# A transformer block on one core: the weights prepared in pieces of 1 MB, and the first token tile in the same stage

## The chip, the cores and the metric

The kernel runs on one core of a Trainium2 chip. The core has five engines that each work through a queue of their own: TensorE (PE, with its weight load PEld), VectorE (DVE), ScalarE (ACT), GpSimd (POOL) and SyncE (SP), which here issues the DMAs. Engines wait for each other by semaphores. The metric is the device time of one execution in microseconds (us), the median of three runs.

## What is computed

A layer norm of x (8 x 1024 x 512), an attention branch on it with 16 heads, a feed-forward branch with ternary weights, and the sum of x and both:

```python
def ternarize_weights(w):
    gamma = jnp.mean(jnp.abs(w))
    return jnp.sign(jnp.round(w / (gamma + EPS))) * gamma
def bitlinear(x, w):
    xn = layer_norm(x)
    ...
    return jnp.einsum('bsd,od->bso', x_hat, w_hat)
...
xn = _layernorm(x, axis=-1)
x = x + _L0_attn_ref(xn, L0_attn_W_qkv, L0_attn_W_o) + _L0_ffn_ref(xn, L0_ffn_w_fc, L0_ffn_w_proj)
```

W_qkv is 1536 x 512 (3 MB), W_o 512 x 512 (1 MB), w_fc 2048 x 512 and w_proj 512 x 2048 (4 MB each), all float32. A ternary weight is 1 above a threshold (gamma + EPS)/2, -1 below its negative, and 0 between, so a matrix can be made ternary only when the mean of its absolute values is known.

## The kernel before

The program is three stages, one after the other, each a block that all engines enter and leave together (a barrier stands between two blocks): `weight_stage`, `token_stage`, `attention_output_stage`.

`weight_stage` (lines 84 to 270) prepares four matrices. SP loads each with one DMA, in the order W_qkv, w_fc, w_proj, W_o (lines 121 to 124). W_qkv: DVE takes the largest absolute value of each partition (line 159), POOL that over the partitions (`partition_all_reduce`, line 147), DVE makes a scale of it (lines 163, 164). PE transposes 128 x 128 blocks, four to a unit of 512 columns in PSUM (line 221), ACT writes the unit as float16 into `wh` (line 255), DVE the rest into `wl` (`low_parts`, line 175). There are 12 units and four PSUM buffers. For the ternary matrices DVE sums the absolute values of w_fc (line 182) and ACT those of w_proj (line 259); POOL adds the partitions; DVE makes the thresholds (lines 185 to 187) and then two passes over the whole matrix, one that compares with the lower threshold (line 190) and one that compares with the upper and subtracts the first result (line 191). Then PE transposes the result, 64 blocks to a matrix (line 228), and ACT copies the 16 units of each to `t1T` and `t2T` (lines 263, 266). W_o is treated as W_qkv was (lines 202 to 210, 242, 270), and at the end PE sums `t2T` over its rows into `colsum` with 16 matmuls against ones (line 247), which DVE copies out (line 212).

`token_stage` (from line 274) works through 16 tiles of 512 tokens. Ahead of its loop it prepares the first tile by itself: SP loads it (line 347), DVE makes its statistics (`stats`, lines 419 to 424), POOL turns them into factors in nine short steps (`norm`, lines 384 to 392), DVE normalises the rows into `x2` (`normed`, line 432), PE transposes them (line 606), ACT writes the high part `xh` (`high`, line 535) and DVE the low part `xl` (`low`, line 448). The second and later tiles are prepared inside the loop's body for the tile before. The body begins on PE with the products of `t1T` and the tile (line 640), then those for q, k and v (line 616), the products of `t2T` (line 652), and so on. `attention_output_stage` follows, with its own buffers.

The order on every engine is the order in which its function is written. What stands in one of these queues waits for all that stands ahead of it.

## Time and profile before

| | us |
|---|---|
| median of 3 runs | 3440.56 |
| lowest, highest | 3439.92, 3441.74 |
| the profiled execution's own time | 3441.16 |
| its span in the profile | 3439.4 |
| PE busy in the span | 3313.1 (96%) |
| DVE, ACT, POOL busy | 2424.7, 1989.6, 1966.8 |
| last instruction of the weight stage (DVE) begins | 78.81 |
| first matmul of the first tile's body (PE) begins | 101.16 |

The profile counts time from the span's start. "Busy" is the time in which an engine works on at least one instruction. A row of a timeline begins with the start and the duration, and ends with the idle time of that engine before it and what ended it. The granted clock of PE is given as a share of 2.4 GHz: 1.00 is 2.4 GHz, 0.50 is 1.2 GHz.

### The profile page before, as it was taken

The page shows a single profiled execution, that of the slowest core. Times are in us where ns is not written, and L with a number is a line of the kernel's source. Part 1 is how long each engine was busy: PE and PEld are TensorE (multiplying, and loading weights), DVE is VectorE, ACT ScalarE, POOL GpSimd, SP SyncE. Part 2 cuts the span into 40 slices and gives each one's busy share as a digit, 9 for nine tenths or more (in the row PEclk, how much of TensorE's full clock was granted, in tenths as well). Part 3 has the DMA queues.
Part 4 walks back from the last instruction along what each step waited for, and adds up shares of the span by engine and source line. Part 5 has one row for each costly group of instructions (what it writes and reads, how often), then busy time and mean ns, then how long its engine had stood idle before and what let it go on. Part 6 is the DMA issues. An engine that isn't in the chain of part 4 may idle for free.

```text
span 3439.4 us, 47929 instructions
## 1 busy us (share of the span) xinstructions
PE 3313.1 (96%) x17648; PEld 1371.8 (40%) x17648; DVE 2424.7 (70%) x3450; ACT 1989.6 (58%) x2949; POOL 1966.8 (57%) x690
## 2 busy tenths in 40 slices
PE   3899999999999999989999999999999999999788
PEld 2444444444444444442333333333333333333233
DVE  6676666666666666668787777877877878776144
ACT  3444444444444444433787777877877878778411
POOL 0322232323232323223999999999999999999600
PEclk8899999999999999996999999999999999999999
DMA  4122222222222222224333333332333333331277
GB/s 169 71 71 94 84 87 78 89 89 89 78 82 94 85 82 78 86 71 84 71 72 79 76 74 71 78 77 67 83 72 67 85 70 67 85 73 42 92 261 255
DMA packets 375958, 307.64 MB, mean 89 GB/s; under 512 B 300672, under 2 KB 317056, under 8 KB 365440
## 3 DMA queue, kind: packets, MB, share of 16 engines
q1 hardware_dynamic: 375744, 304.69, 31.9%
q8 instruction: 146, 2.39, 0.3%
q14 instruction: 68, 0.56, 0.1%
HBM read 96.99 MB, written 139.46 MB: 69 GB/s over the span
## 4 chain that ended last, share of the span: by engine, by line
PE 46%; DMA 3%; DVE 2%; issue 1%; POOL 1%; ACT 1%; SPq 0%; POOLq 0%; ACTq 0%; DVEq 0%
PE es_for_maxima_and_scores L1058 14%; PE outputs L1049 14%; PE es_for_maxima_and_scores L1037 13%; PE misc L1082 5%; DMA k_stackT<-attention_scratch 2%; DMA out<-q_stackT 2%; DVE half_maxima L973 1%; POOL probs_sum L894 1%; PE es_for_maxima_and_scores L1115 1%; DVE q_stackT L1009 0%; ACT k_stackT L932 0%; ACT probs L926 0%; DVE q_stackT L1015 0%; DMA q_stackT<-stack_scratch 0%; PE misc L1066 0%
## 5 line engine op out<-in xcount | busy, mean ns | idle before, releaser
L973 DVE TENSOR_REDUCE half_maxima<-es_for_maxima_and_scores 128x1 f32<-128x512 f32 x2048 | 1275.6, 682 | 324.4 <-PE es_for_maxima_and_scores L1058 324.3
L926 ACT ACTIVATE probs<-es_for_maxima_and_scores,scalars 128x512 f32<-128x512 f32 x2048 | 1253.6, 692 | 379.7 <-PE es_for_maxima_and_scores L1037 377.2
L894 POOL TENSOR_TENSOR probs_sum<-probs_sum,probs 128x2048 f32<-128x2048 f32 x256 | 1164.0, 4547 | 27.8
L1058 PE MATMUL es_for_maxima_and_scores<-k_stackT,q_stackT 96*128 96x512 f16 x2048 | 800.4, 392 | 12.1 <-DMA q_stackT<-stack_scratch 11.1
L1037 PE MATMUL es_for_maxima_and_scores<-q_stackT,k_stackT 98*128 98x512 f16 x2048 | 778.2, 383 | 5.9 <-ACT probs L926 4.5
L1049 PE MATMUL outputs<-probs,v_rows 128*32 128x512 f32 x4096 | 541.1, 600 | 3.1 <-ACT probs L926 0.8
L402 POOL TENSOR_TENSOR gelu_sum<-gelu_sum,gelu_out 128x1024 f32<-128x1024 f32 x96 | 254.8, 2654 | 451.5 <-ACT gelu_out L577 451.5
L1058 PEld LDWEIGHTS es_for_maxima_and_scores<-k_stackT,q_stackT 96*128 96x128 f16 x2048 | 199.7, 98 | 603.9 <-DVE half_maxima L973 447.4
L640 PE MATMUL psA<-x_hi,ternary_fcT 128*128 128x512 f16 x1024 | 389.9, 381 | 1.4 <-DVE x_lo L448 1.4
L640 PE MATMUL psA<-x_lo,ternary_fcT 128*128 128x512 f16 x1024 | 389.8, 381 | 0.0
L652 PE MATMUL psC<-ternary_projT,h_lo 128*128 128x512 f16 x1024 | 388.0, 379 | 0.0
L652 PE MATMUL psC<-ternary_projT,h_hi 128*128 128x512 f16 x1024 | 388.0, 379 | 0.0
L894 POOL TENSOR_TENSOR probs_sum<-probs 128x2048 f32<-128x2048 f32 x64 | 291.2, 4550 | 154.5 <-ACT probs L926 154.5
L1037 PEld LDWEIGHTS es_for_maxima_and_scores<-q_stackT,k_stackT 98*128 98x128 f16 x2048 | 294.8, 145 | 211.9 <-ACT probs L926 31.6
L577 ACT ACTIVATE gelu_out<-psA,scalars 128x1024 f32<-128x1024 f32 x128 | 142.7, 1115 | 347.9 <-PE psA L640 347.9
L402 POOL TENSOR_TENSOR gelu_sum<-gelu_out 128x1024 f32<-128x1024 f32 x16 | 41.0, 2564 | 489.5 <-ACT gelu_out L577 489.5
L471 DVE TENSOR_SCALAR h_hi<-gelu_out,scalars 128x1024 f16<-128x1024 f32 x128 | 186.5, 1457 | 161.0 <-ACT gelu_out L577 157.3
L616 PE MATMUL psB<-wqkvT_hi,x_hi 128*128 128x512 f16 x768 | 291.1, 379 | 0.0
L616 PE MATMUL psB<-wqkvT_lo,x_hi 128*128 128x512 f16 x768 | 291.1, 379 | 0.0
L616 PE MATMUL psB<-wqkvT_hi,x_lo 128*128 128x512 f16 x768 | 291.1, 379 | 0.0
L557 ACT ACTIVATE hi_hi_lo_hi_rows<-psB,qkv_scale 128x1024 f16<-128x1024 f32 x192 | 214.0, 1115 | 127.2 <-PE psB L616 127.2
L535 ACT CAST x_hi<-psB 128x512 f16<-128x512 f32 x64 | 34.5, 588 | 335.6 <-PE psB L606 335.6
(126 smaller groups left out, 3175.8 us busy)
## 6 DMA issues: line engine op xcount, KB each, us to landing
stack_scratch<-hi_hi_lo_hi_rows SPq DMA_DIRECT2D x32, 1536.0 KB, 5.1
stack_scratch<-hi_hi_lo_hi_rows SPq DMA_DIRECT2D x32, 576.0 KB, 6.0
v_scratch<-v_rows_out SPq DMA_DIRECT2D x32, 576.0 KB, 6.9
x_rows<-in_L_attn_x SPq DMA_DIRECT2D x16, 1024.0 KB, 4.8
x_plus_ffn_scratch<-x_rows SPq DMA_DIRECT2D x16, 1024.0 KB, 3.9
v_rows<-v_scratch SPq DMA_DIRECT2D x32, 512.0 KB, 4.0
inverse_denominators<-denominators_scratch SPq DMA_DIRECT2D x256, 64.0 KB, 2.0
attention_scratch<-out_normed SPq DMA_DIRECT2D x64, 256.0 KB, 2.1
```

The costliest lines, as they stand in the source:

```text
L402: nc.gpsimd.tensor_tensor(gacc[:], g[:, 0, :] if j == 1 else gacc[:], g[:, j % 4, :], ALU.add).then_inc(g_added, 1)
L471: nc.vector.tensor_scalar(hh[:, pair, :], gj, S["inv1"], None, ALU.mult).then_inc(hh_ready, 1)
L557: nc.scalar.activation(stack[:, i % 2, heads, 0:2, :], rows.unsqueeze(2).to_broadcast([P, BANK // DH, 2, DH]), ACT.Copy, scale=rc[:, s, i: ...
L616: last = nc.tensor.matmul(psB[:, u % 2, :], xx[:, s, c, i * P:(i + 1) * P], keep[ww][:, c, cols], start=(k == 0), stop=(k == len(terms) - 1))
L640: last = nc.tensor.matmul(psA[:, 2 * (j % 2) + b, :], w, xx[:, s, c, :], start=(c == 0 and k == 0), stop=(c == CD - 1 and k == 1))
L652: last = nc.tensor.matmul(psC[:, i % 2, :], h[:, f, i * P:(i + 1) * P], keep["t2T"][:, f, :], start=(f == 0 and k == 0), stop=(f == CF - 1 ...
L894: nc.gpsimd.tensor_tensor(acc[:, hf], pr[:, 0] if j == 1 else acc[:, hf], pr[:, j], ALU.add).then_inc(added, 1)
L926: nc.scalar.activation(pr[:, w % 8, h, :], psS[:, bank(g, HG * w + h), :], ACT.Exp, scale=keep["scal"]["escale"]).then_inc(exp_done, 1)
L973: nc.vector.tensor_reduce(mx[:, slot(n, 2), h, t, kh:kh + 1], psX[:, bank(n, r), :], axis=AX.X, op=ALU.max).then_inc(max_done, 1)
L1037: nc.tensor.matmul(psS[:, bank(g, HG * w + h), :], kT[0:AUG, slot(g, 4), h, i:L:KT_N], qT[0:AUG, slot(g, 4), h, hf * BANK:(hf + 1) * BANK] ...
L1049: last = nc.tensor.matmul(psO[32 * h:32 * h + 32, :], v[:, slot(g, 2), h, i, :], pr[:, w % 8, h, :], start=(i == 0), stop=(i == KT_N - 1))
L1058: nc.tensor.matmul(psX[:, bank(n, r), :], qT[0:STACK, slot(n, 4), h, t * P:(t + 1) * P], kT[0:STACK, slot(n, 4), h, kh * BANK:(kh + 1) * B ...
```

## The change

**Loads.** W_qkv and w_fc come in pieces of 1 MB, each with a semaphore of its own; the first tile of x is loaded between them into `xs`, which with `xh`, `xl`, `bn`, `mv`, `sm`, `rc` and their semaphores now lives in `keep` through both stages. W_o and w_proj (four pieces) are issued only when PE has transposed all of W_qkv, because W_o and the normalised tile `x2` take the place of W_qkv's rows.

**W_qkv.** The largest absolute value is taken piece by piece; the units run in the order of the pieces.

**The first tile.** Its statistics stand on DVE after six of the twelve low parts, its factors on POOL after the first reduction over partitions, its transposes on PE behind the W_qkv units, its high part on ACT and its low part on DVE between pieces of w_fc. The same code is taken out of `token_stage`.

**Sums.** ACT sums the absolute values of both matrices, in eight pieces; DVE adds four partial sums of each.

**Ternary weights.** DVE no longer subtracts. Two comparisons of a piece give two float16 indicators: `above` (a buffer of its own, used for both matrices) and `below` (written over the float32 piece that it is made of, 4 x 512 with gaps). PE makes the transposed difference in PSUM: for each block a matmul of `above` with the identity and one of `below` with the negative identity, accumulated. PSUM for it is float32.

**Column sums.** They are interleaved with w_proj's units, two behind.

```diff
+            for k in range(THIRDS):
+                sp.dma_start(wqkv[:, piece(k)], rows[:, piece(k)]).then_inc(ld_qkv[k], 16)
+            sp.dma_start(xs[:, 0], x_v[0]).then_inc(x_loaded[0], 16)
...
+            sp.wait_ge(full32, N32)
+            sp.dma_start(wo, W_o.rearrange("(j p) d -> p j d", p=P)).then_inc(ld_o, 16)
...
-                link(nc.vector.tensor_scalar(tern_rows, flat, thr[:, thr0 + 1:thr0 + 2], None, ALU.is_lt))
-                nc.vector.scalar_tensor_tensor(tern_rows, flat, thr[:, thr0:thr0 + 1], tern_rows,
-                                               ALU.is_gt, ALU.subtract).then_inc(tern, 1)
...
+            def fc_piece(k):
+                nc.vector.tensor_scalar(above[:, piece(k), :], wfc[:, piece(k), :], thr[:, 1:2], None, ALU.is_gt)
+                nc.vector.tensor_scalar(fc_below[:, piece(k), :], wfc[:, piece(k), :], thr[:, 0:1], None,
+                                        ALU.is_lt).then_inc(tern, 1)
...
+                for r in range(4):
+                    nc.tensor.matmul(pst[:, u % 3, r * P:(r + 1) * P], plus[r], id16[:], start=True, stop=False)
+                    last = nc.tensor.matmul(pst[:, u % 3, r * P:(r + 1) * P], minus[r], nid16[:], start=False, stop=True)
                 last.then_inc(full16, 1)
...
+            for f in range(CF):
+                k, q = divmod(f, 4)
+                if q == 0:
+                    pe.wait_ge(tern, 4 + k + 1)
...
+                difference(CF + f, [above[:, 4 * k + r, cols] for r in range(4)], [proj_below[:, r, k, cols] for r in range(4)])
+                if f >= 2:
+                    column_sum(f - 2)
+            column_sum(CF - 2)
+            column_sum(CF - 1)
```

In `token_stage` the first tile's load, `norm(0, 0)`, `stats(0, 0)`, `normed(0, 0)`, `low`, `high` and `transposes` ahead of the loop go.

What stands on DVE from the low parts of W_qkv to the second matrix, before:

```order
L175 SCALAR_TENSOR_TENSOR wqkvT_lo<-weight_psum,scalars,wqkvT_hi 128x512 [waits hi_out] x11
L182 TENSOR_REDUCE per_partition<-wfc_rows 128x1 [waits loaded_fc]
L185 TENSOR_SCALAR scalars<-over_partitions 128x1 [waits reduced]
L186 TENSOR_SCALAR thresholds<-scalars 128x1 [waits vector_step]
L187 TENSOR_SCALAR thresholds<-thresholds 128x1 [waits vector_step]
L190 TENSOR_SCALAR ternary_fc_rows<-wfc_rows,thresholds 128x8192 [waits vector_step]
L191 SCALAR_TENSOR_TENSOR ternary_fc_rows<-wfc_rows,thresholds,ternary_fc_rows 128x8192 [waits vector_step]
```

The same place now; `wqkv_rows` in row L256 is `x2`, and `wfc_rows` as an output is `below`:

```order
L203 SCALAR_TENSOR_TENSOR wqkvT_lo<-weight_psum,scalars,wqkvT_hi 128x512 [waits hi_out] x6
L256 TENSOR_SCALAR wqkv_rows<-tile_xs,tile_mv,tile_sm 128x512 [waits mv_ready,pool_step]
L256 TENSOR_SCALAR wqkv_rows<-tile_xs,tile_mv,tile_sm 128x512 x3
L208 TENSOR_REDUCE per_partition_sums<-per_partition 128x1 [waits parts]
L211 TENSOR_SCALAR scalars<-over_partitions 128x1 [waits reduced]
L212 TENSOR_SCALAR thresholds<-scalars 128x1 [waits vector_step]
L213 TENSOR_SCALAR thresholds<-thresholds 128x1 [waits vector_step]
L216 TENSOR_SCALAR above_threshold<-wfc_rows,thresholds 128x2048 [waits vector_step]
L217 TENSOR_SCALAR wfc_rows<-wfc_rows,thresholds 128x4x512
L216 TENSOR_SCALAR above_threshold<-wfc_rows,thresholds 128x2048
L217 TENSOR_SCALAR wfc_rows<-wfc_rows,thresholds 128x4x512
L265 TENSOR_TENSOR tile_xl<-weight_psum,tile_xh 128x512 [waits xh_ready] x4
```

The sum of absolute values has left DVE, the tile's normalising stands ahead of the thresholds, and its low part between the second and the third piece.

ACT in the whole weight stage, before:

```order
L255 ACTIVATE wqkvT_hi<-weight_psum,scalars 128x512 [waits full32] x11
L259 ACTIVATE ternary_proj_rows,per_partition<-wproj_rows 128x8192 [waits loaded_proj]
L263 COPY ternary_fcT<-weight_psum 128x512 [waits full16] x16
L266 COPY ternary_projT<-weight_psum 128x512 [waits full16] x16
L270 ACTIVATE woT_hi<-weight_psum,wo_scale 128x512 [waits wo_full,wo_scaled]
L270 ACTIVATE woT_hi<-weight_psum,wo_scale 128x512 [waits wo_full] x3
```

And now, from the last units of W_qkv on:

```order
L352 ACTIVATE wqkvT_hi<-weight_psum,scalars 128x512 [waits full32] x4
L356 ACTIVATE above_threshold,per_partition<-wfc_rows 128x2048 [waits loaded_fc1]
L356 ACTIVATE above_threshold,per_partition<-wfc_rows 128x2048 [waits loaded_fc2]
L356 ACTIVATE above_threshold,per_partition<-wfc_rows 128x2048 [waits loaded_fc3]
L380 CAST tile_xh<-weight_psum 128x512 [waits t_full] x4
L368 CAST ternary_fcT<-ternary_psum 128x512 [waits full16] x8
L363 ACTIVATE wqkv_rows,per_partition<-wproj_rows 128x2048 [waits loaded_proj0]
L363 ACTIVATE wqkv_rows,per_partition<-wproj_rows 128x2048 [waits parts,loaded_proj1]
L368 CAST ternary_fcT<-ternary_psum 128x512 [waits full16] x8
L363 ACTIVATE wqkv_rows,per_partition<-wproj_rows 128x2048 [waits parts,loaded_proj2]
L363 ACTIVATE wqkv_rows,per_partition<-wproj_rows 128x2048 [waits parts,loaded_proj3]
L392 ACTIVATE woT_hi<-weight_psum,wo_scale 128x512 [waits wo_full,wo_scaled]
```

The sums over w_proj, which stood ahead of all the copies of `t1T`, now stand between and behind them, and W_o's high part ahead of the copies of `t2T`.

## Rows read from the trace of the kernel before

**Rows 1.** Page: busy time, share of the span, instructions of each engine.

```profile
PE 3313.1 (96%) x17648; PEld 1371.8 (40%) x17648; DVE 2424.7 (70%) x3450; ACT 1989.6 (58%) x2949; POOL 1966.8 (57%) x690
```

**Rows 2.** Stretches: length, busy PE, PEld, DVE, ACT, POOL; PE clock, DMA share, GB/s.

```profile
0.00:79.50 79.50, 28.38 (x208) 21.16 (x208) 58.11 (x41) 34.06 (x51) 5.88 (x18) 0.81 0.42 158
295.00:502.00 207.00, 207.00 (x993) 97.89 (x992) 143.11 (x156) 94.63 (x107) 66.01 (x40) 1.00 0.27 90
```

**Rows 3.** Timeline from W_qkv's landing to the first sum; start, duration, engine, line.

```profile
12.21 6.55 DVE L159 TENSOR_REDUCE per_partition<-wqkv_rows 128x1 f32<-128x6144 f32 x1 [12.21 <-DMA wqkv_rows<-in_L_attn_W_qkv]
...
18.90 0.38 POOL L147 PARTITION_ALL_REDUCE over_partitions<-per_partition  x1 [16.43 <-DVE per_partition L159]
...
20.50 8.62 DVE L175 SCALAR_TENSOR_TENSOR wqkvT_lo<-weight_psum,scalars,wqkvT_hi 128x512 f16<-128x512 f32 x12 [0.27 <-ACT wqkvT_hi L255]
...
25.02 3.00 ACT L255 ACTIVATE wqkvT_hi<-weight_psum,scalars 128x512 f16<-128x512 f32 x5 [0.17 <-PE weight_psum L221]
...
29.04 8.68 DVE L182 TENSOR_REDUCE per_partition<-wfc_rows 128x1 f32<-128x8192 f32 x1
```

**Rows 4.** Timeline, the sum on ACT and the passes over both matrices on DVE.

```profile
32.98 7.03 ACT L259 ACTIVATE ternary_proj_rows<-wproj_rows 128x8192 f16<-128x8192 f32 x1 [4.96 <-DMA wproj_rows<-in_L_ffn_w_proj]
...
38.81 4.49 DVE L190 TENSOR_SCALAR ternary_fc_rows<-wfc_rows,thresholds 128x8192 f16<-128x8192 f32 x1
...
43.33 8.75 DVE L191 SCALAR_TENSOR_TENSOR ternary_fc_rows<-wfc_rows,thresholds,ternary_fc_rows 128x8192 f16<-128x8192 f32 x1
...
57.20 8.75 DVE L191 SCALAR_TENSOR_TENSOR ternary_proj_rows<-wproj_rows,thresholds,ternary_proj_rows 128x8192 f16<-128x8192 f32 x1
```

**Rows 5.** Timeline, the second matrix's transposes, copies and column sums.

```profile
66.00 3.53 PEld L228 LDWEIGHTS weight_psum<-id,ternary_proj_rows 128*128 128x128 f16 x32 [6.48 <-DVE ternary_proj_rows L191]
...
66.65 7.93 ACT L266 COPY ternary_projT<-weight_psum 128x512 f16<-128x512 f16 x16 [5.93 <-PE weight_psum L228]
...
75.15 3.62 PE L247 MATMUL colsum_psum<-ternary_projT,ones 128*128 128x512 f16 x16
75.20 2.73 DVE L209 SCALAR_TENSOR_TENSOR woT_lo<-weight_psum,wo_scale,woT_hi 128x512 f16<-128x512 f32 x4 [5.59 <-ACT woT_hi L270]
78.81 0.69 DVE L212 COPY ternary_proj_sums<-colsum_psum 128x512 f32<-128x512 f32 x1 [0.88 <-PE colsum_psum L247]
```

**Rows 6.** Timeline, the first token tile's preparation and the body's start.

```profile
79.78 0.34 SPq L347 DMA_DIRECT2D x_rows<-in_L_attn_x  x1
...
85.08 2.47 DVE L419 BATCH_NORM_STATS2 bn<-x_rows 128x6 f32<-128x512 f32 x4 [5.58 <-DMA x_rows<-in_L_attn_x]
...
89.17 0.19 POOL L384 TENSOR_TENSOR norm_small<-mean_var,powers_and_epsilons 128x4 f32<-128x4 f32 x1 [20.00 <-issue]
...
93.30 1.91 DVE L432 TENSOR_SCALAR x_normed<-x_rows,mean_var,norm_small 128x512 f32<-128x512 f32 x4 [5.34 <-POOL qkv_scale L392]
...
101.16 0.61 PE L640 MATMUL psA<-x_hi,ternary_fcT 128*128 128x512 f16 x1 [1.40 <-DVE x_lo L448]
...
107.48 0.38 PE L616 MATMUL psB<-wqkvT_hi,x_hi 128*128 128x512 f16 x1
108.83 0.75 DVE L471 TENSOR_SCALAR h_hi<-gelu_out,scalars 128x1024 f16<-128x1024 f32 x1 [7.73 <-ACT gelu_out L577]
```

**Rows 7.** Stretches of 2 or 3 us, columns as in rows 2.

```profile
66.00:68.00 2.00, 1.99 (x19) 1.77 (x20) 1.93 (x4) 1.35 (x3) 0.00 (x0) 0.50 0.00 0
...
70.00:72.00 2.00, 1.63 (x19) 0.90 (x16) 0.00 (x0) 2.00 (x6) 0.00 (x0) 1.00 0.00 0
...
101.00:104.00 3.00, 2.84 (x7) 1.04 (x8) 0.10 (x1) 0.68 (x1) 0.00 (x0) 0.50 0.00 0
```

**Rows 8.** Line 353, loads of tiles 2 to 16: issue (ns, first and last start), landing.

```profile
L353 SPq DMA_DIRECT2D x_rows<-in_L_attn_x x15: 340/372/425, 80.2 to 1366.7; - x15
...
DMA to landing us min/median/max: 4.7/4.8/7.3
```

**Rows 9.** Line 147: the changes of POOL's configuration ahead of the all-reduces.

```profile
L147 POOLq MODIFY_POOL_CONFIG  x2: 11/11/11, 2.4 to 2.4; - x2
```

More of the change, by code:

```diff
@@ L80, in wait, with weight_stage @@
         eng.wait_ge(sem, value)
-def weight_stage(nc, W_qkv, W_o, w_fc, w_proj, keep):
+def weight_stage(nc, x_v, W_qkv, W_o, w_fc, w_proj, keep):
     n_w = F * D
@@ new lines, in _ @@
+            last.then_inc(mv_ready, 1)
+            for u in range(6, N32):
+                low_part(u)
+            dve.wait_ge(pool_step, 9)
+            dve.wait_ge(mv_ready, 1)
+            for i in range(4):
+                last = nc.vector.tensor_scalar(x2[:, i, :], xs[:, 0, i, :], mv[:, i, 0:1], sm[:, 6, i:i + 1],
+                                               ALU.subtract, ALU.mult)
+            last.then_inc(x2_ready, 1)
+            thresholds(FC, 4, S["gamma1"], 2, 4)
+            fc_piece(0)
@@ new lines, in _ @@
+            fc_piece(1)
+            for c in range(CD):
+                dve.wait_ge(xh_ready, c + 1)
+                nc.vector.tensor_tensor(xl[:, 0, c, :], ps[:, c, :], xh[:, 0, c, :], ALU.subtract).then_inc(xl_ready, 1)
+            fc_piece(2)
+            fc_piece(3)
+            dve.wait_ge(ld_o, 16)
+            nc.vector.tensor_reduce(sums[:, 2:3], wo, axis=AX.XY, op=ALU.max, apply_absolute_value=True).then_inc(summed, 1)
+            thresholds(PROJ, 12, S["gamma2"], 4, 8)
+            proj_piece(0)
@@ L267, in _ @@
+            for u in range(8):
+                fc_out(u)
+            proj_sum(0)
+            proj_sum(1)
+            for u in range(8, CF):
+                fc_out(u)
+            proj_sum(2)
+            proj_sum(3)
             act.wait_ge(wo_scaled, 1)
@@ L588, in body @@
                     high(shift(t, 1), 1 - s, range(CD))
-            high(0, 0, range(CD))
             steps(act, body)
@@ L659, in body @@
                         transposes(shift(t, 1), 1 - s, (2 * i - 2, 2 * i - 1))
-            transposes(0, 0, range(CD), first=True)
             steps(pe, body)
```

281 lines of the change are left out of this document (171 added, 110 removed).

## The prediction, made before the changed kernel had run

> **What bounds the kernel now.** I read the page first: PE is busy 96% of the span [rows 1], so DVE's 70% tells little. The stretches say where some of the missing 4% is: in a stretch of over two token tiles PE is busy 207.0 of 207.0 us at full clock, in the first 79.5 us only 28.4 [rows 2]. The change touches nothing but the time before the first tile's body, which begins at 101.16. Behind that PE does not stop in the token stage, so an earlier start passes on to the end one for one. The timeline gives the chain that sets the 101 us. W_qkv lands at 12.2; DVE reduces it for 6.55 us, then works without a real pause to 66: low parts 8.62, sum of w_fc 8.68 [rows 3], then 4.49 + 8.75 us for each ternary matrix [rows 4]. After 66 come PE's transposes with ACT's copies, W_o, the column sums to 78.77, DVE's last copy to 79.50 [rows 5]. Then the first tile starts from nothing: load 5.3, statistics, 5.34 us of waiting for POOL, normalising, transposes: 21.7 us in which nothing else runs [rows 6].
>
> **The change part by part** (times are those of the profiled execution, from its start).
>
> Head. The large loads land at a pace. W_qkv ends a wait at 12.2, w_proj one at 33.0, with 8 MB between them: 2.6 us for each 1 MB. Counted from 12.2 the pieces of W_qkv land near 7.0, 9.6, 12.2, then x at 14.8 and w_fc at 17.4, 20.0, 22.6, 25.2 [rows 3, 4]. DVE needs 6.55/3 = 2.2 us for a piece and ends at 14.4 instead of 18.76. From that end to the first low part it was 1.74 us; with one more small sum of 0.15 the low parts begin at 16.3, 4.2 earlier.
>
> Low parts and the tile. Six low parts (8.62/12 = 0.72 each) to 20.7, statistics 2.5 plus some 0.6 for the aggregates to 23.9, six more to 28.3. POOL's factors take 5.3 us from the statistics [rows 6], to 29.2, under the low parts; normalising 1.9, to 31.1. ACT has the high parts (0.60 each, five in 3.00 [rows 3]) and the sum over w_fc's first piece; it is free near 27. A sum over 8192 columns was 7.03 us [rows 4]; over 2048 that is 1.76 and a fixed part, 2.0. Three more: 33.0. So DVE waits 2 us for ACT, and normalising is free. The tile's transposes on PE (from 31.1) and its four high parts on ACT (behind the sums, to about 36) end before the first piece of w_fc is ready, and cost nothing.
>
> First thresholds. From the end of DVE's sum (37.72) to the first pass (38.81) lay 1.09 us [rows 3, 4]; with the small sum the first comparison begins at 34.3.
>
> Comparisons. 8192 columns took 4.49, 1024 took 0.75 [rows 4, 6], so 2048 take 0.75 + 1024 x 0.00052 = 1.28 us, 1.23 back to back: 2.45 a piece, 19.6 for eight. Before, the two passes of both matrices were 26.5 and DVE's sum 8.7. That is the size of the idea: 15.6 us less on DVE, against 64 + 64 more small matmuls on PE. w_fc's pieces are ready at 36.8 and 39.2, then the tile's low parts (4 x 0.7, hidden, as will be seen), 44.5 and 46.9; W_o's maximum to 49.2.
>
> ACT becomes the bound. Its queue now is: 8 copies of `t1T`, two sums over w_proj, 8 copies, two sums. The eighth copy needs piece 2 (39.2) and PE. A weight load of 128 columns comes each 3.53/32 = 0.11 us at 1.2 GHz [rows 5, 7]; a unit of 8 matmuls is 0.88 us there and half of that, 0.44, at 2.4 GHz. The eighth copy ends at 41.7 (fast) to 44.5 (slow); I take 43.0. Then 4.0 (two sums), 4.8 (8 x 0.60; before, from float16 PSUM, 7.93/16 = 0.50 [rows 5], but the float32 row is the nearer one), 4.0: 55.8. w_proj's pieces are issued when PE has finished W_qkv, about 26.2; 5.3 us for W_o [rows 6] and 2.6 for each piece give 42.0 for the last, so their late issue is hidden by 10 us.
>
> Second thresholds at 55.8 + 0.2 + 1.1 = 57.1. DVE: four pieces 9.8, W_o's scale 0.5, W_o's low parts 2.7 [rows 5]: last piece at 70.1. ACT copies `t2T` from 62.6 on (W_o's high parts are ahead of it), 16 x 0.60 = 9.6, to 72.2 at the earliest. PE does a unit and a column sum in 0.44 + 0.22 = 0.66, so behind the last piece 4 x 0.66 = 2.6, a copy 0.67, two column sums 0.6, DVE's copy 0.73 [rows 5]: stage end 74.7; I take 75.0 instead of 79.5. Only 4.5 us: the 15.6 saved on DVE come back as ACT's sums and a longer chain of copies.
>
> Passage to the token stage. DVE's end to SP's first DMA was 0.28 us, the shortest it can be [rows 5, 6]; POOL's first step there began 1.2 us after the statistics that it waited for (89.17 against 93.30 - 5.34 = 87.96) [rows 6]. I take 0.9 of 0.3 to 1.5. PE begins the body at 75.9 instead of 101.16: 25.3.
>
> Clock. The 16 matmuls from 101.16 to 107.48 took 6.3 us, at 1.2 GHz [rows 6, 7]; at 2.4 GHz 16 x 0.216 = 3.5 (the column sums: 15 in 3.62 - 0.38 [rows 5]). PE will have worked almost without a gap from 63 to 74, and in the like place before it had reached 1.00 four us after it began and kept it [rows 7]. That gives 2.8 more, and would not if it fell. The Trainium skill (TensorE: Matmul & The Clock Gate, HAM clock gate) says that the low clock is the default state and that activity releases it. By that page the added matmuls help, and the row agrees (0.50 in 66 to 68, 1.00 in 70 to 72).
>
> **Sum:** 25.3 + 2.8 = 28.1 us off 3441.16, which is 3413.1 by the profiled execution; the median stands 0.6 below that one, 3412.5. I round to 3413.
>
> Against the pieces speaks the Trainium skill (DMA: Bandwidth & Descriptors, Anatomy of one DMA), which puts a fixed cost of about 2 us on each DMA; there are 9 more in this stage, x's among them. The trace shows two DMAs of 1 MB issued 0.4 us apart that landed 5.3 and 7.3 us after issue [rows 6, 8], 2.4 us apart, no more than the pace of the large ones. Paid one behind another it would be 4 us on W_qkv's last piece, and the sum would be 24 instead of 28; by the row it is nothing.
>
> **Rivals.**
> 1. PE's clock stays low where the kernel now leans on it. PE idles between w_fc's last unit (about 52) and w_proj's first (60). Then the eighth copy is 1.5 later, units with their column sum take 1.3 instead of 0.66 from 63 on (13 of them, 17 us, stage end 7.5 later), and the first tile's 2.8 are not won: 28.1 - 1.5 - 7.5 - 2.8 = 16.3, 3424. Against: before, 3.5 us of dense transposes were enough [rows 5, 7]. Chance 0.12.
> 2. The second comparison, written with gaps over its own input, runs at the pace of the two-input pass, 8.75/8192 [rows 4], 2.3 instead of 1.2 us. Two of w_fc's and four of w_proj's lie on the chain: 6.6 later, 3419. No row has such an output. Chance 0.10.
> 3. POOL now changes its configuration three times around the tile's factors. The change before the first all-reduce is issued at 2.4 and the all-reduce runs at 18.90, when its data are there [rows 3, 9], so it may cost anything up to 16.4 us. In the new order it has 4 us between the factors (29.2) and the sum over w_fc (33.2): 0 to 12 later, up to 3425. Chance 0.08.
> 4. The change doesn't shorten the stage: ACT's and PE's hand-overs eat the 4.5 us and it ends at 79.5; the tile alone gives 20.8 + 2.8 = 23.6, 3417. Chance 0.05.
> 5. Slower than before: the tile's buffers lie elsewhere in memory for all 16 tiles. If PE's reads or the writers of `xh`, `xl` became slower by more than 28.1/16 = 1.8 us a tile, the kernel would lose. A tile takes (1366.7 - 80.2)/14 = 92 us [rows 8]: 2% is the point of no gain, 3% would be 3413 + 44 = 3457. Against: the body's code is the same and PE has no idle time in it [rows 2]. Chance 0.03.
>
> **How the numbers follow.** The forecast has 0.62. Its own unknowns: passage 0.3 to 1.5, eighth copy 41.7 to 44.5, clock behind the last piece (4 x 1.3 instead of 4 x 0.66, 2.6 us more): 3409 to 3419. The range 3409 to 3424 takes in rivals 2 and 4, about half of 1 and of 3, and leaves out 5. A measurement of this kernel can tell 0.2%, 7 us. All cases but the fifth are at least 15 us faster: faster 0.96, within 0.2% 0.01, slower 0.03.
>
> **What would show it.** First low part at 16.3; first comparison at 34.3, behind ACT's sum of piece 3; a comparison 1.2 to 1.3 us in both forms; DVE idle from about 49 to 57, ended by ACT's last sum; last comparison at 70; DVE's copy of the column sums ending at 75; body at 76 with matmuls 0.216 apart from the start; the rest shifted as a whole. I am wrong if DVE's second wait is ended by POOL or a DMA, if a comparison lasts over 2 us, or if a token tile's length changes.

## The result, and the profile after

| | before | after |
|---|---|---|
| median of 4 runs each, us | 3440.24 | 3419.32 |
| lowest, highest | 3436.09, 3441.74 | 3417.53, 3421.41 |
| the profiled execution, its span | 3441.16, 3439.4 | 3417.53, 3415.7 |
| ratio of times | | 0.9941 [0.9928, 0.9954] |
| body of the first tile begins on PE | 101.16 | 79.37 |

The kernel is 20.9 us faster, and the interval leaves out no change. The time lies inside the range; it is 6.3 us above the forecast of 3413.0. (The four runs of before are the three of the beginning and one beside the changed kernel.)

The page of after: PE is still what bounds the span; it gained 5 us of busy time by the added matmuls, and DVE lost 17 [rows 1].

```profile
PE 3318.2 (97%) x17776; PEld 1381.0 (40%) x17776; DVE 2407.6 (70%) x3466; ACT 1997.6 (58%) x2963; POOL 1963.7 (57%) x692
```

DVE in the weight stage, after (columns as in [rows 3]). L216 and L222 are the comparisons that give `above`, L217 and L223 those that give `below`, L208 the small sum, L211 the first step of the thresholds, L256 the tile's normalising, L287 the last copy. Comparisons of the later pieces are left out.

```profile
9.18 2.29 DVE L228 TENSOR_REDUCE per_partition<-wqkv_rows 128x1 f32<-128x2048 f32 x1 [0.38 <-DMA wqkv_rows<-in_L_attn_W_qkv]
...
16.17 4.35 DVE L203 SCALAR_TENSOR_TENSOR wqkvT_lo<-weight_psum,scalars,wqkvT_hi 128x512 f16<-128x512 f32 x6 [0.27 <-ACT wqkvT_hi L352]
...
29.09 1.91 DVE L256 TENSOR_SCALAR wqkv_rows<-tile_xs,tile_mv,tile_sm 128x512 f32<-128x512 f32 x4 [1.85 <-POOL tile_rc L185]
31.75 0.16 DVE L208 TENSOR_REDUCE per_partition_sums<-per_partition 128x1 f32<-128x4 f32 x1 [0.75 <-ACT above_threshold L356]
39.10 0.15 DVE L211 TENSOR_SCALAR scalars<-over_partitions 128x1 f32<-128x1 f32 x1 [7.20 <-POOL over_partitions L163]
...
39.66 1.29 DVE L216 TENSOR_SCALAR above_threshold<-wfc_rows,thresholds 128x2048 f16<-128x2048 f32 x1
40.87 1.28 DVE L217 TENSOR_SCALAR wfc_rows<-wfc_rows,thresholds 128x2048 f16<-128x2048 f32 x1
...
60.33 0.16 DVE L208 TENSOR_REDUCE per_partition_sums<-per_partition 128x1 f32<-128x4 f32 x1 [6.42 <-ACT wqkv_rows L363]
...
61.56 1.29 DVE L222 TENSOR_SCALAR above_threshold<-wproj_rows,thresholds 128x2048 f16<-128x2048 f32 x1
...
78.36 0.69 DVE L287 COPY ternary_proj_sums<-colsum_psum 128x512 f32<-128x512 f32 x1 [3.74 <-PE colsum_psum L318]
```

POOL in the same stretch: its first and last step for the tile's factors, and the all-reduce for w_fc.

```profile
24.96 0.19 POOL L177 TENSOR_TENSOR tile_sm<-tile_mv,powers_and_epsilons 128x4 f32<-128x4 f32 x1 [10.02 <-issue]
...
28.85 0.20 POOL L185 TENSOR_TENSOR tile_rc<-tile_sm,powers_and_epsilons 128x4 f32<-128x4 f32 x1
38.67 0.40 POOL L163 PARTITION_ALL_REDUCE over_partitions<-per_partition_sums  x1 [9.61 <-issue]
```

The changes of POOL's configuration ahead of the all-reduces (L163) and of the factors (L177), as their issue is recorded:

```profile
L163 POOLq MODIFY_POOL_CONFIG  x4: 10/10/11, 2.8 to 29.3; - x4
```

```profile
L177 POOLq MODIFY_POOL_CONFIG  x2: 82/82/83, 14.9 to 14.9; - x2
```

What is to be seen: DVE has the sum over w_fc at 31.9, three thresholds' steps from its comparisons, and waits 7.20 us for POOL. POOL does nothing in that time: its all-reduce is released by "issue", not by DVE. Its last factor ends at 29.05, the change is issued at 29.3, and the all-reduce runs 9.4 us after that. The change takes 10 ns in its own row; its cost stands in the next row's idle time. The other change, issued at 14.9 ahead of the factors, cost 10.02 us. Normalising waits for it only from 27.2 to 29.1, but it isn't wholly hidden: the statistics were there at 23.3 and the factors began at 24.96. So the change back was issued some 1.6 us later than it could have been, and these are part of the 7.20.

ACT after that wait, and PE at the start of the first tile's body:

```profile
45.84 2.60 ACT L368 CAST ternary_fcT<-ternary_psum 128x512 f16<-128x512 f32 x5 [0.27 <-PE ternary_psum L313]
48.29 1.95 ACT L363 ACTIVATE wqkv_rows<-wproj_rows 128x2048 f16<-128x2048 f32 x1
...
52.33 3.97 ACT L368 CAST ternary_fcT<-ternary_psum 128x512 f16<-128x512 f32 x8
...
70.00 7.87 ACT L395 CAST ternary_projT<-ternary_psum 128x512 f16<-128x512 f32 x12 [0.63 <-PE ternary_psum L313]
```

```profile
79.37 0.38 PE L750 MATMUL psA<-tile_xh,ternary_fcT 128*128 128x512 f16 x1 [1.05 <-PEq L86]
79.59 0.38 PE L750 MATMUL psA<-tile_xl,ternary_fcT 128*128 128x512 f16 x1
```

ACT copies `t1T` (L368), sums over w_proj (L363), copies again, sums again; DVE's second wait of 6.42 us is for that. Then W_o (L392) and `t2T` (L395). DVE's last copy ends at 79.05 and PE begins the body at 79.37, with matmuls 0.22 apart at once [rows 6: 6.3 us for sixteen; here 3.45].

PE's clock in four stretches (columns as in [rows 2]):

```profile
36.00:41.00 5.00, 0.00 (x0) 0.00 (x0) 1.80 (x5) 0.00 (x0) 0.40 (x1) 0.50 0.77 326
40.00:46.00 6.00, 3.79 (x37) 3.80 (x38) 6.00 (x7) 1.92 (x4) 0.00 (x0) 0.51 0.01 4
66.00:68.00 2.00, 1.55 (x12) 1.01 (x11) 2.00 (x4) 2.00 (x5) 0.00 (x0) 0.50 0.00 0
70.00:72.00 2.00, 2.00 (x28) 1.67 (x27) 2.00 (x3) 1.77 (x4) 0.00 (x0) 1.00 0.00 0
```

PE had nothing to do from 36 to 41 and began w_fc's transposes at 0.51 of full clock, and w_proj's, from 64.1 on, at 0.50.

### The profile page after: what moved, and what is told of

It is laid out like the page before. It is cut to its first block, busy times and chain, and to the rows that moved or that the text cites. A ratio compares the mean times of both kernels' runs of the same rounds, so it can differ in the third digit from the quotient of the medians.

```text
span 3415.7 us, 48244 instructions
## 1 busy us (share of the span) xinstructions
PE 3318.2 (97%) x17776; PEld 1381.0 (40%) x17776; DVE 2407.6 (70%) x3466; ACT 1997.6 (58%) x2963; POOL 1963.7 (57%) x692
## 3 DMA queue, kind: packets, MB, share of 16 engines
q1 hardware_dynamic: 375872, 304.69, 31.9%
## 4 chain that ended last, share of the span: by engine, by line
PE 47%; DMA 3%; DVE 2%; issue 1%; POOL 1%; ACT 1%; SPq 0%; POOLq 0%; ACTq 0%; DVEq 0%
PE es_for_maxima_and_scores L1167 14%; PE outputs L1158 14%; PE es_for_maxima_and_scores L1146 13%; PE misc L1191 5%; DMA k_stackT<-attention_scratch 1%; DMA out<-q_stackT 1%; DVE half_maxima L1082 1%; POOL probs_sum L1003 1%; PE es_for_maxima_and_scores L1224 1%; DVE q_stackT L1118 0%; ACT k_stackT L1041 0%; ACT probs L1035 0%; DVE q_stackT L1124 0%; DMA q_stackT<-stack_scratch 0%; PE misc L1175 0%
## 5 line engine op out<-in xcount | busy, mean ns | idle before, releaser
L1167 PE MATMUL es_for_maxima_and_scores<-k_stackT,q_stackT 96*128 96x512 f16 x2048 | 800.3, 391 | 12.2 <-DMA q_stackT<-stack_scratch 11.2
L750 PE MATMUL psA<-tile_xh,ternary_fcT 128*128 128x512 f16 x1024 | 388.2, 379 | 1.3 <-PEq L86 1.1
L750 PE MATMUL psA<-tile_xl,ternary_fcT 128*128 128x512 f16 x1024 | 388.1, 379 | 0.0
L726 PE MATMUL psB<-wqkvT_lo,tile_xh 128*128 128x512 f16 x768 | 291.1, 379 | 0.0
L726 PE MATMUL psB<-wqkvT_hi,tile_xl 128*128 128x512 f16 x768 | 291.1, 379 | 0.0
L726 PE MATMUL psB<-wqkvT_hi,tile_xh 128*128 128x512 f16 x768 | 291.1, 379 | 0.0
L668 ACT ACTIVATE hi_hi_lo_hi_rows<-psB,tile_rc 128x1024 f16<-128x1024 f32 x192 | 213.8, 1113 | 127.4 <-PE psB L726 127.4
L646 ACT CAST tile_xh<-psB 128x512 f16<-128x512 f32 x60 | 32.2, 588 | 314.5 <-PE psB L716 314.5
```

Of the source, the lines that this page charges most:

```text
L668: nc.scalar.activation(stack[:, i % 2, heads, 0:2, :], rows.unsqueeze(2).to_broadcast([P, BANK // DH, 2, DH]), ACT.Copy, scale=rc[:, s, i: ...
L726: last = nc.tensor.matmul(psB[:, u % 2, :], xx[:, s, c, i * P:(i + 1) * P], keep[ww][:, c, cols], start=(k == 0), stop=(k == len(terms) - 1))
L750: last = nc.tensor.matmul(psA[:, 2 * (j % 2) + b, :], w, xx[:, s, c, :], start=(c == 0 and k == 0), stop=(c == CD - 1 and k == 1))
L1167: nc.tensor.matmul(psX[:, bank(n, r), :], qT[0:STACK, slot(n, 4), h, t * P:(t + 1) * P], kT[0:STACK, slot(n, 4), h, kh * BANK:(kh + 1) * B ...
```

## The experiments

The question was what the missing 3.5 us of the body's start are: the forecast was 75.9. The comparison that opens the chain is 5.4 us late, and a change of POOL's configuration stands in front of it. The runs take that change apart (1 to 3), then the other parts of the change (4 to 6), and then use what was found (7, 8). Runs 1, 2, 3 and 5 were made together with the kernel before at 3439.39 (one run), the others with it at 3438.79 (nine runs). A time without an interval is that of one run, and is read together with its trace.

### 1. w_proj's loads behind the all-reduce

```diff
+            sp.wait_ge(reduced, 2)
             rows = w_proj.rearrange("(j p) f -> p j f", p=P)
             for k in range(4):
```

> w_proj's four loads wait until POOL has added w_fc's sums over the partitions, so no DMA traffic runs between W_o's landing (about 31) and that all-reduce. In the changed kernel POOL's configuration change is issued at 29.3 and the all-reduce runs at 38.67, while its data are there at 31.9 and the DMA queue is full until 39. Theory A (a configuration change takes a fixed 9 to 10 us): the all-reduce runs at 38 to 39 again. Theory B (its code waits behind w_proj's packets in the DMA queues): the all-reduce runs at 31.9 to 33. Under either the body begins later than 79.4, since w_proj lands late: under A w_proj's last piece at about 38.7 + 13 = 52, which ACT's last sum (58.3) still hides, so the body at 79 to 81; under B at about 74.

Measured: 3414.48 us, the body at 79.20. (The time is 3.1 us below the profiled execution of the changed kernel, with a body that begins only 0.2 earlier; the rest lies in the attention stage and the projection, whose code is the same. One run doesn't show that the edit did it.) The queues of DMA, first in the changed kernel from 29.3 to 38.8, then here from 30 to 37 (a digit is the busy share of the 16 DMA engines in a fortieth of the window):

```profile
DMA  9999989998899999988999999979999899979999
```

```profile
DMA  1000000000000000000000000000000000000000
```

And POOL's last factor and its all-reduce here:

```profile
30.17 0.20 POOL L186 TENSOR_TENSOR tile_rc<-tile_sm,powers_and_epsilons 128x4 f32<-128x4 f32 x1
36.31 0.40 POOL L164 PARTITION_ALL_REDUCE over_partitions<-per_partition_sums  x1 [5.94 <-issue]
```

With the DMA engines idle the all-reduce comes 5.94 us after the last factor instead of 9.61. So neither pure case holds: 5.9 us belong to the change of configuration itself, and 3.7 go with the traffic beside it, w_proj's four pieces. The first comparison is at 37.32, only 2.3 us earlier than after, because the change ahead of the factors took 11.32 us here instead of 10.02. And the body begins only 0.2 earlier. The gain is lost behind the comparison:

```profile
43.49 0.59 ACT L369 CAST ternary_fcT<-ternary_psum 128x512 f16<-128x512 f32 x1 [0.27 <-PE ternary_psum L314]
44.34 0.59 ACT L369 CAST ternary_fcT<-ternary_psum 128x512 f16<-128x512 f32 x1 [0.27 <-PE ternary_psum L314]
```

ACT's copies of `t1T` stand 0.85 us apart, each waiting for PE at half clock, up to the seventh (in the changed kernel up to the fourth), and three more do so in the second half. ACT's last sum ends at 60.0 against 60.3. PE's pause ahead of these copies was shorter than in the changed kernel (4.0 us instead of 7.5), and the half clock behind it lasted longer; the traces don't say why.

### 2. The totals of both ternary matrices on PE

```diff
-            reduce(FC, bass.bass_isa.ReduceOp.add)
             reduce(2, bass.bass_isa.ReduceOp.max)
-            reduce(PROJ, bass.bass_isa.ReduceOp.add)
...
-                dve.wait_ge(reduced, summed_to)
+                dve.wait_ge(pe_total, summed_to)
...
+            def add_partitions(k):
+                pe.wait_ge(summed, k + 1)
+                nc.tensor.matmul(psw[:, k:k + 1], ones_sq[:], sums[:, k:k + 1], start=True, stop=True).then_inc(pe_total, 1)
```

`ones_sq` is 128 x 128 ones in float32; the product gives every partition the sum over all. The matmul for w_fc stands behind the first unit of the tile's transposes, that for w_proj ahead of its first unit.

> The sums of both ternary matrices are added over the partitions by one float32 matmul with ones on PE; POOL keeps the two maxima, so its second configuration change has from 29 to 54 to finish. Theory (the all-reduce for w_fc is what was late): first comparison at about 33.0 instead of 39.66, since the sum is ready at 31.91 and matmul, PSUM read and three small steps take about 1.1. The chain behind it on ACT moves up with it, 6 to 6.7 us, so the body begins at 72.7 to 73.4 instead of 79.37. Rival (something else in the chain, such as ACT's sums over w_proj waiting for their DMA, takes over): first comparison at 33 but ACT's sums end less than 3 us earlier than 60.3 and the body begins at 76 or later. w_proj's last piece lands at 39, before ACT would ask for it at about 51, so I expect the first.

Measured: 3408.99 us, the body at 72.21, 7.2 earlier than after. DVE, and the stretch 36 to 41:

```profile
32.93 0.16 DVE L211 TENSOR_SCALAR scalars<-colsum_psum 128x1 f32<-128x1 f32 x1 [0.68 <-PE colsum_psum L304]
...
33.50 1.29 DVE L216 TENSOR_SCALAR above_threshold<-wfc_rows,thresholds 128x2048 f16<-128x2048 f32 x1
...
54.44 1.29 DVE L222 TENSOR_SCALAR above_threshold<-wproj_rows,thresholds 128x2048 f16<-128x2048 f32 x1
```

```profile
36.00:41.00 5.00, 3.92 (x64) 3.58 (x64) 5.00 (x7) 4.06 (x10) 0.00 (x0) 1.00 0.83 347
```

The total is there 0.68 us after the small sum, and the first comparison begins at 33.50, 6.2 us earlier. That is 0.8 before the forecast's 34.3. The other 1.0 us goes with PE: it passes from the tile's transposes to w_fc's with little pause, the clock is 1.00 where it was 0.51, and ACT ends its first eight copies 7.6 us after the first comparison instead of 8.8. The rival, by which ACT's sums would hold the body at 76 or later, is out.

### 3. Six changes of configuration with nothing beside them

```diff
             reduce(PROJ, bass.bass_isa.ReduceOp.add)
+            for n in range(3):
+                nc.gpsimd.tensor_tensor(extra[:, 4 * n:4 * n + 4], keep["powers"][:, 4:8], keep["powers"][:, 4:8], ALU.add)
+                nc.gpsimd.partition_all_reduce(extra[:, 12 + n:13 + n], sums[:, 0:1], P, bass.bass_isa.ReduceOp.max)
```

The results go to a tile that nothing reads.

> Behind POOL's last all-reduce stand three more pairs of an ordinary step on 128x4 and an all-reduce on 128x1, into a scratch tile that nothing reads, in the stretch from 61 on in which no DMA runs. Theory A (each change of configuration takes 9 to 10 us by itself): starts of the six steps lie about 9 to 10 us apart, 55 to 60 us in all, and the token stage begins that much later than the other engines need (body at about 120). Theory B (a change is short unless DMA traffic delays it): the six steps lie under 2 us apart, and the body begins at 79 to 80. A mixed outcome would be one direction short and one long.

Measured: 3441.86 us, the body at 104.40, since the stage can't end before POOL. POOL, the all-reduce for w_fc and then the added chain:

```profile
40.32 0.40 POOL L164 PARTITION_ALL_REDUCE over_partitions<-per_partition_sums  x1 [9.60 <-issue]
...
70.24 0.19 POOL L192 TENSOR_TENSOR extra<-powers_and_epsilons 128x4 f32<-128x4 f32 x1 [7.63 <-issue]
76.22 0.38 POOL L193 PARTITION_ALL_REDUCE extra<-per_partition_sums  x1 [5.78 <-issue]
...
97.21 0.19 POOL L192 TENSOR_TENSOR extra<-powers_and_epsilons 128x4 f32<-128x4 f32 x1 [6.65 <-issue]
103.68 0.38 POOL L193 PARTITION_ALL_REDUCE extra<-per_partition_sums  x1 [6.27 <-issue]
```

Both forms of the expectation were wrong: a change is neither short nor 9 to 10 us. Each is issued 0.4 us after the start of the instruction before it; to an ordinary step it costs 6.7 to 7.6 us of idle time, to an all-reduce 5.8 to 6.3. In the stretch with w_proj's traffic it is 9.60 again, and 11.63 to the tile's factors under w_fc's. The Trainium skill (GPSIMD Engine Reference, Instruction dispatch) says that the first call of a freshly loaded kernel pays a load of code of about 6 us that no row of a profile shows; the all-reduces of this chain agree, with 5.8 to 6.3, and the ordinary steps lie above it, with 6.7 to 7.6. That the time grows under traffic is what runs 1 and 3 show beside it. It would if the code came through the same DMA engines; that it does isn't shown.

PE stood idle for 24 us ahead of this body, and its first matmuls are 0.43 apart. From the body's start to the attention stage it took 1448.3 us, against 1446.6 in the changed kernel: so a start at half clock costs 1.7 us here (2.3 by the kernel before, with 1448.9), where the forecast had 2.8.

### 4. DVE subtracts, in pieces

```diff
-                nc.vector.tensor_scalar(above[:, piece(k), :], wfc[:, piece(k), :], thr[:, 1:2], None, ALU.is_gt)
-                nc.vector.tensor_scalar(fc_below[:, piece(k), :], wfc[:, piece(k), :], thr[:, 0:1], None,
-                                        ALU.is_lt).then_inc(tern, 1)
+                link(nc.vector.tensor_scalar(above[:, piece(k), :], wfc[:, piece(k), :], thr[:, 0:1], None, ALU.is_lt))
+                nc.vector.scalar_tensor_tensor(above[:, piece(k), :], wfc[:, piece(k), :], thr[:, 1:2], above[:, piece(k), :],
+                                               ALU.is_gt, ALU.subtract).then_inc(tern, 1)
```

The same for w_proj; PE then makes one matmul for each block instead of two.

> The changed kernel with the ternary matrices made as before, by two passes of DVE that end in a subtraction, but still piece by piece (a comparison of 1.28 us and a two-input pass of 2048 x 8.75/8192 = 2.2 to 2.3), and one matmul for each block on PE instead of two. Theory (DVE's time for a piece lies on the chain for six of the eight pieces, PE's added matmuls lie beside it): w_fc's pieces end about 3.5 apart instead of 2.4; ACT's last sum over w_proj ends at about 62 instead of 60.3; the four pieces of w_proj add 4 x 1.1; PE's units are shorter, 0.44 with a column sum instead of 0.66, which gives back about 1. The body begins at 83 to 85 instead of 79.37. Rival (what PE pays eats what DVE saves): the body begins at 78.5 to 80.5. POOL's configuration change can move either by up to 2.

Measured: 3424.73 us, the body at 88.42, 9.0 later than after (1.0 of it is a first comparison at 40.67, behind changes of 10.68 and 9.82 us). DVE, and the last stretch of the stage:

```profile
40.67 1.29 DVE L216 TENSOR_SCALAR above_threshold<-wfc_rows,thresholds 128x2048 f16<-128x2048 f32 x1
42.00 2.35 DVE L217 SCALAR_TENSOR_TENSOR above_threshold<-wfc_rows,thresholds,above_threshold 128x2048 f16<-128x2048 f32 x1
...
87.40 0.69 DVE L287 COPY ternary_proj_sums<-colsum_psum 128x512 f32<-128x512 f32 x1 [4.08 <-PE colsum_psum L317]
```

```profile
78.00:87.40 9.40, 7.09 (x42) 3.96 (x42) 5.22 (x7) 4.50 (x8) 0.00 (x0) 0.64 0.00 0
```

A piece takes 3.58 us instead of 2.40, the old pair of passes made 3.3 of it by [rows 4]. That is most of it. From the first comparison of w_fc to ACT's last sum it takes 2.9 us more than in the changed kernel, and from the first comparison of w_proj to the end of DVE's last piece (82.9) 4.8 more, with DVE at work throughout. The stretch that is left, from there to DVE's copy, takes 4.5 us against 4.2. The body is still 3 to 5 us behind what was expected: 1.0 is POOL's, the sums are 1.2 later than was reckoned, and the shorter units of PE, which were to give back 1, gave nothing. Most of ACT's copies of `t2T` from 73.5 on start 0.85 us behind the one before, the last at 86.13; the clock granted from 78 to 87.4 is 0.64, where the changed kernel has 1.00 for its last copies. So the added matmuls, besides sparing DVE a slow pass, came with a higher clock, but little of the 9.0 us is the clock's. Whether the number of matmuls or the shorter pauses went with it isn't separated by this run.

### 5. The first tile prepared in the token stage, as before

```diff
-            sp.dma_start(xs[:, 0], x_v[0]).then_inc(x_loaded[0], 16)
             rows = w_fc.rearrange("(j p) d -> p j d", p=P)
...
-            pool.wait_ge(mv_ready, 1)
-            link(nc.gpsimd.tensor_tensor(v1, var, keep["powers"][:, 4:8], ALU.add))
...
+            norm(0, 0)
             steps(pool, body)
```

Also the tile's steps on DVE, PE and ACT go back; the pieces and the indicators stay.

> The changed kernel with the first tile prepared in the token stage, as in the kernel before; the pieces and the difference on PE stay. Theory A: without the tile's factors there is no configuration change between POOL's all-reduces, so w_fc's all-reduce runs when its data are ready. ACT's sums move up by about 1 us (DVE's statistics no longer between the low parts), so the first comparison at about 32.5; DVE has no low parts of x between pieces. Stage end 79.05 - 7 = 71 to 72. Then the tile costs what it did, 101.16 - 79.50 = 21.7, so the body begins at 92.5 to 94 at the lower clock: 7 to 9 us earlier than before, 13 to 15 later than with the tile inside, that is about 3433. If instead the all-reduce is late again, near 38, Theory A is wrong.

Measured: 3429.80 us, the body at 94.13, 3 us less than was expected. DVE (L190 is the first step of the thresholds, L501 the normalising), and the body:

```profile
32.03 0.15 DVE L190 TENSOR_SCALAR scalars<-over_partitions 128x1 f32<-128x1 f32 x1 [0.53 <-POOL over_partitions L162]
...
71.74 0.69 DVE L248 COPY ternary_proj_sums<-colsum_psum 128x512 f32<-128x512 f32 x1 [3.57 <-PE colsum_psum L273]
77.75 2.47 DVE L488 BATCH_NORM_STATS2 tile_bn<-tile_xs 128x6 f32<-128x512 f32 x4 [5.31 <-DMA tile_xs<-in_L_attn_x]
```

```profile
94.13 0.39 PE L709 MATMUL psA<-tile_xh,ternary_fcT 128*128 128x512 f16 x1 [1.40 <-DVE tile_xl L517]
94.36 0.38 PE L709 MATMUL psA<-tile_xl,ternary_fcT 128*128 128x512 f16 x1
```

The change has two halves of unequal size. The weight stage alone ends at 72.43 instead of 79.50: 7.1 us. The tile inside it brings 94.13 - 79.37 = 14.8. It is less than the 21.7 us that the passage took before [rows 6], because the tile's steps cost the stage 79.05 - 72.43 = 6.6 us there. Without them no ordinary step of POOL stands between the all-reduces, DVE waits 0.53 us for the total instead of 7.20, and the first comparison is at 32.60. The change of configuration is thus a price of moving the tile, and the largest one.

The last two rows show something else. The sixteen matmuls of this body are 0.22 us apart from the second on, at full clock, as in the changed kernel, though the tile is prepared in the token stage as before, PE transposes it from 5.9 us ahead of the body as it did there, with the same pauses of 0.55 us between two halves and 1.40 ahead of the body, and was idle for 16.6 us ahead of all that. In the kernel before the clock stayed at 0.50 until the body had run for nearly 6 us. So the same work of PE ended at either level, and it isn't shown that the full clock at the changed kernel's body, some 2 of its 20.9 us, comes from moving the tile.

### 6. W_qkv and w_fc by one DMA each

```diff
-            for k in range(THIRDS):
-                sp.dma_start(wqkv[:, piece(k)], rows[:, piece(k)]).then_inc(ld_qkv[k], 16)
+            sp.dma_start(wqkv[:], rows).then_inc(ld_qkv[0], 16)
...
-            for k in range(4):
-                sp.dma_start(wfc[:, piece(k)], rows[:, piece(k)]).then_inc(ld_fc[k], 16)
+            sp.dma_start(wfc[:], rows).then_inc(ld_fc[0], 16)
```

> The changed kernel with W_qkv loaded by one DMA of 3 MB and w_fc by one of 4 MB; the reductions stay in three parts, and all else too. Theory: DVE's first reduction begins at 12.2 instead of 6.5, its three parts end at 19.0 instead of 14.15, the first low part begins at 21.0 instead of 16.2. All behind it moves by 4.8: POOL's all-reduce, its change to the ordinary configuration (which takes 7 to 11 us from there and so holds the tile's factors), the factors, the change back. The first comparison at 43.5 to 46 and the body at 83 to 85.5. Rival (the pieces gain nothing because POOL's changes of configuration and ACT's sums set the time later on): the body below 81.

Measured: 3419.55 us, the body at 82.43, 3.1 later. (By the time alone nothing would be seen: it is one run, and lies inside the changed kernel's 3417.53 to 3421.41.) DVE:

```profile
11.99 6.67 DVE L226 TENSOR_REDUCE per_partition<-wqkv_rows 128x1 f32<-128x2048 f32 x3 [11.99 <-DMA wqkv_rows<-in_L_attn_W_qkv]
...
20.68 4.35 DVE L201 SCALAR_TENSOR_TENSOR wqkvT_lo<-weight_psum,scalars,wqkvT_hi 128x512 f16<-128x512 f32 x6 [0.27 <-ACT wqkvT_hi L350]
...
43.23 1.29 DVE L214 TENSOR_SCALAR above_threshold<-wfc_rows,thresholds 128x2048 f16<-128x2048 f32 x1
```

The pieces bring 4.5 us at the first low part (16.17 against 20.68), as the sum had it (4.2). W_qkv's last piece lands at 11.86 in the changed kernel, and the whole matrix at 11.99 here: two more DMAs in front of it cost nothing. Of the 4.5 us the first comparison keeps 3.6 (39.66 against 43.23) and the body 3.1. Both are earlier than was expected (43.5 to 46 and 83 to 85.5): the change ahead of the factors, issued at 19.4, did not hold them. They began at 27.92, released by DVE's statistics after 8.46 us of idle time, so this change took no more than that, though w_fc's load filled the DMA engines until about 24.4.

### 7. One version on top of run 2, and run 2 again

Run 7 is run 2 with w_proj's last piece summed by DVE, which waits at that time, and with W_o's high and low parts moved behind the first eight copies of `t2T`.

```diff
-            thresholds(PROJ, 12, S["gamma2"], 2, 8)
+            dve.wait_ge(ld_proj[3], 16)
+            nc.vector.tensor_reduce(part[:, 15:16], wproj[:, 3, :], axis=AX.X, op=ALU.add,
+                                    apply_absolute_value=True).then_inc(last_sum, 1)
+            dve.wait_ge(last_sum, 1)
+            thresholds(PROJ, 12, S["gamma2"], 2, 7)
...
-            proj_sum(3)
+            for f in range(8):
+                proj_out(f)
             act.wait_ge(wo_scaled, 1)
```

> The kernel with the totals on PE and two edits more: DVE, which idles from 47.7 to 54 there while ACT sums, takes the last piece of w_proj's sum (2.3 us), and W_o's high and low parts stand behind the first eight copies of w_proj and behind its last piece. Theory: ACT's sums end 2.1 earlier, second thresholds 2.1 earlier, first comparison of w_proj at about 53.0 instead of 55.2; the copies of w_proj begin with the first piece instead of 2.4 us of W_o later, and PE's 16 units and column sums (0.66 each, the first at half clock) run from 55.7 on without a stall, to 68. The body begins at 68 to 70 instead of 72.21, and the kernel takes 3404 to 3409 at the median. Rival (PE's low clock at the start of w_proj costs what the earlier start gains): the body at 70.5 to 72.

Measured, five runs: 3407.62 us (3406.76 to 3409.58), ratio to before 0.9911 [0.9897, 0.9924]; the body at 70.86. DVE and ACT (L384 copies `t2T`, L409 is W_o's high part):

```profile
47.68 2.27 DVE L271 TENSOR_REDUCE per_partition<-wproj_rows 128x1 f32<-128x2048 f32 x1
...
52.24 1.29 DVE L222 TENSOR_SCALAR above_threshold<-wproj_rows,thresholds 128x2048 f16<-128x2048 f32 x1
```

```profile
56.71 0.59 ACT L384 CAST ternary_projT<-ternary_psum 128x512 f16<-128x512 f32 x1 [0.27 <-PE ternary_psum L324]
57.56 0.59 ACT L384 CAST ternary_projT<-ternary_psum 128x512 f16<-128x512 f32 x1 [0.27 <-PE ternary_psum L324]
...
64.58 4.78 ACT L384 CAST ternary_projT<-ternary_psum 128x512 f16<-128x512 f32 x8
```

w_proj's first comparison is at 52.24, 2.2 us earlier than in run 2, and its last piece ends at 62.2. Yet the body is only 1.4 earlier, where the rival had it (70.5 to 72) and not at 68 to 70. The first copies stand 0.85 apart again, from 55.85 on; PE is busy only 1.2 of the 4 us from 52 to 56, at 0.56 of full clock, and stays at 0.58 to 60. And behind the last piece eight copies and W_o are still to come, 7 us of ACT. What each of the two edits brings by itself isn't separated.

Run 8 is the kernel of run 2 with more rounds.

> The kernel with the totals of both ternary matrices on PE again, timed. Its one run took 3408.99 with the body at 72.21, 7.2 earlier than in the changed kernel (median 3419.3 of four runs). Theory: 3410 to 3413 at the median, since the change of configuration no longer holds the chain. Its spread between runs is also expected to shrink from 3.9 us to what the kernel before shows in its undisturbed runs, about 2, if part of the changed kernel's spread comes from the length of that change.

Measured, four runs: 3409.06 us (3407.53 to 3409.69), ratio 0.9914 [0.9899, 0.993]; the body at 72.67. That is 0.9 below the range that was expected. So it is 29.7 us below the kernel before, where the changed kernel was 20.9 below (each against the runs of before beside it). Run 7 is 1.4 us below run 8 on the same chip, and the two ranges overlap: that it is better is read from the body's start, 1.4 and 1.8 us earlier than in the two traces of run 2's kernel, and not from the time.

## Why the prediction was right, and where it missed

**What bounds the kernel: right.** From the body's first matmul to the first of the attention stage it took 1448.9 us before and 1446.6 after, the attention stage 1618.5 and 1619.6, the projection 198.2 and 197.5 (each from its first matmul to its last). An earlier start passes on to the end, and the tile's length did not change (rival 5 is out).

**Head and low parts: right.** The reductions begin at 6.51, 9.18 and 11.86 (forecast 7.0, 9.6, 12.2), the first low part at 16.17 (16.3), normalising at 29.09 (29.2), ACT's sums of w_fc end at 31.7 (33.0). Run 6 shows the 4.2 us of the pieces as 4.5. Nothing was paid for the pieces of W_qkv. (The Trainium skill, DMA: Bandwidth & Descriptors, Anatomy of one DMA, which the prediction held against them, gives its 2 us for DMAs that GpSimd issues; here SP issues them.)

**First thresholds: the step that failed.** "With the small sum the first comparison begins at 34.3": it began at 39.66, 5.4 late. The step took DVE's sum as the last thing to wait for. It was POOL's change of configuration, rival 3, which had 0.08. The rival named the place, the 4 us that it had (2.9 by the trace) and a bound of 0 to 12; 7.20 us of waiting came true. What spoke for a higher chance stood in the trace of the kernel before already. The bound of "up to 16.4" came from a change that had all the time it wanted [rows 9]. But the first tile's factors in the kernel before began 9.3 us after their change of configuration was issued, on entry to the token stage, and 1.2 us after their data were there; the row ends in [20.00 <-issue] [rows 6]. The change, in the kernel before:

```profile
L384 POOLq MODIFY_POOL_CONFIG  x2: 11/11/11, 79.9 to 79.9; - x2
```

So that row was a change of configuration on the path, and it gave its length. With 9.3 us instead of none the sum would have put the first comparison near 39.8 and the body near 81. The 1.2 us were read as the passage to the stage, and so the same error stands twice in the forecast, there with the other sign: the passage was 0.32 us, where 0.9 was taken.

**Comparisons: right.** 1.28 us each, 1.20 apart, both forms, so rival 2 is out. By run 4 the old pair would have been 3.58 a piece.

**ACT becomes the bound: right, with two sizes off.** DVE's second wait, 6.42 us, is ended by ACT. From the first comparison of w_fc to that of w_proj it took 21.9 us, forecast 22.8: the eighth copy ended 8.8 after (8.7), the first two sums took 4.0, and eight copies took 3.97 instead of 4.8. The float32 rows that I had taken for the copies [rows 3] are scaled writes, 0.69 each in the trace; a plain copy takes 0.58, and behind one another they start about 0.49 apart, as from float16.

**The end of the stage.** From w_proj's first comparison to DVE's last copy 17.5 us, forecast 17.9; PE was below full clock until about 70, as in rival 1, but only for the first units (0.50 in 66 to 68), and it had 1.00 in 70 to 72 and in the body. What shows of rival 1 are two waits of ACT for PE, 0.58 and 0.63, where it had priced 7.5.

**Clock of the first body: right in its number, not shown in its cause.** 3.45 us for sixteen matmuls against 3.5, and 6.3 before, so 2.8 us saved there; 2.3 of them are left at the attention stage. The prediction laid it to PE's work without a gap ahead of the body. Run 3, with 24 us of idle PE, has the slow start. But run 5 has the fast one with the same pauses and transposes that ended at half clock in the kernel before. So this term may be luck.

**The sum.** By the profiled executions 3413.1 was forecast and 3417.53 measured, 4.4 more. 3.5 is the body's start: + 5.4 for the first thresholds, - 0.9 up to the second, - 0.4 up to the stage's end, - 0.6 for the passage. The other 0.9 lies behind the body's start, where 2.8 us were to be saved and 1.9 were (2.3 up to the attention stage, - 1.1 in it, + 0.7 in the projection). It is within what is not explained there: in six profiles with the same code there (before, after, runs 1, 2, 3 and 5) the attention stage took 1618.2 to 1619.6 us and the projection 195.4 to 198.2. The median stands 1.8 above the profiled execution, where I had put it 0.6 below. That is the rest of the 6.3, less the 0.5 by which 3412.5 was rounded up. The changed kernel's times scatter by 3.9 us and run 8's by 2.2, but the nine runs of the kernel before scatter by 4.1 too, so nothing here lays the scatter to the changes of configuration.

## What to carry to other kernels

Look for the releaser "issue" on POOL, and for changes of its configuration in the queue: where ordinary steps and all-reduces alternate, each turn cost POOL 6 to 12 us here that no instruction shows, and it is on the path when less than that lies between the last step and the next one's data. Move one of the two kinds to another engine (here a float32 matmul against ones, 0.68 us) before moving anything else. And when a stage has pauses on PE, reckon what follows them at both clocks: an earlier start upstream gave back 2.3 us as 0.2 (run 1, half clock up to the seventh copy) or 6.2 as 7.2 (run 2, full clock). Which level it will be, one trace doesn't tell: the same preparation of the first tile ended at 0.50 in the kernel before and at 1.00 in run 5.
